# Down projections of the experts: from full-precision products to three fp32r products of split operands, in a one-core decoder layer

## The reference

```python
scores = softmax(x @ gate_w)                       # 8 experts, the best 2 kept and renormalised
for e in range(8):                                 # D = 256, H = 128
    hid = silu(x @ w_gate[e]) * (x @ w_up[e])      # [512, 256]
    y = y + w_per_expert[:, e:e+1] * (hid @ w_down[e])
shared = silu(x @ ws_gate) * (x @ ws_up) @ ws_down
out = x_residual + y + shared
```

## Time and profile before

| | us |
|---|---|
| Median of 3 runs | 206.36 |
| Range of the 3 runs | 206.1 to 208.32 |
| The profiled execution's own time | 206.29 |
| Its span, first to last instruction | 204.4 |
| TensorE busy in the span | 192.2 (94%) |
| VectorE busy | 157.7 (77%) |
| ScalarE busy | 137.1 (67%) |
| GpSimd busy | 97.4 (48%) |

### The profile page before, as it was taken

How to read it: one execution, slowest core, us unless ns; L and a number is a source line. 1 busy time by engine, 2 the same in 40 slices (tenths; PEclk the granted TensorE clock), 3 DMA queues, 4 the chain that set the end, 5 groups by cost and what they waited for, 6 DMA issues and landing times.

```text
span 204.4 us, 4606 instructions
## 1 busy us (share of the span) xinstructions
PE 192.2 (94%) x1626; PEld 150.7 (74%) x1626; DVE 157.7 (77%) x417; ACT 137.1 (67%) x316; POOL 97.4 (48%) x145
## 2 busy tenths in 40 slices
PE   7999996999999799996999999999989999999995
PEld 7688775678767567863666757576658799999994
DVE  2579989687669787579999999999983866458844
ACT  2499857797679749279998898987985332462220
POOL 7599207747673887905769991003400017500330
DMA  5980406801555104679514100000000000000001
GB/s 177 384 198 3 154 2 201 267 0 31 65 63 59 21 7 119 87 105 143 143 34 120 25 2 0 3 2 3 0 0 3 5 0 0 3 0 13 3 0 39
DMA packets 13286, 12.69 MB, mean 62 GB/s; under 512 B 1057, under 2 KB 11297, under 8 KB 13265
## 3 DMA queue, kind: packets, MB, share of 16 engines
q1 hardware_dynamic: 12160, 11.15, 24.2%
q10 hardware_dynamic: 1008, 1.06, 1.6%
q0 software_dynamic: 96, 0.20, 0.7%
HBM read 10.96 MB, written 1.44 MB: 61 GB/s over the span
## 4 chain that ended last, share of the span: by engine, by line
PE 63%; DVE 13%; ACT 10%; issue 6%; POOL 3%; DMA 3%; SPq 1%; DVEq 0%; POOLq 0%; ACTq 0%
PE ps L958 13%; PE ps L919 8%; PE ps L982 8%; PE ps L845 7%; PE ps L861 6%; PE ps L896 5%; PE ps L817 4%; PE ps L878 4%; DVE qk_low L1098 4%; ACT q_t L646 3%; PE ps L742 3%; DMA wk<-in_L_xattn_Wk 3%; DVE q_t L1186 2%; PE ps L936 2%; ACT place_k L646 2%
## 5 line engine op out<-in xcount | busy, mean ns | idle before, releaser
L1186 DVE CUSTOM_DVE_ANT_0 q_t<-ps,mask_add 128x512 f32<-128x512 f32 x64 | 41.4, 684 | 3.4 <-PE ps L878 2.2
L496 POOL TENSOR_TENSOR prob<-prob,rec 128x512 f32<-128x512 f32 x32 | 32.5, 1038 | 22.8 <-DVE rec L1245 22.8
L610 ACT ACTIVATE prob<-ps,low 128x256 f32<-128x256 f32 x64 | 29.8, 491 | 10.3 <-DVE low L1176 10.3
L646 ACT ACTIVATE q_t<-q_t,low 128x512 f32<-128x512 f32 x44 | 29.3, 717 | 4.2 <-DVE low L1186 4.1
L1176 DVE TENSOR_REDUCE low<-ps 128x2 f32<-128x512 f32 x32 | 20.4, 683 | 7.4 <-PE ps L817 7.3
L919 PEld LDWEIGHTS ps<-ident,q_t 128*128 128x128 f32 x176 | 19.6, 141 | 8.7 <-ACT q_t L646 2.9
L532 POOL TENSOR_TENSOR place_k<-place_k 128x256 f32<-128x256 f32 x10 | 7.3, 732 | 38.7 <-DVE place_k L1211 38.7
L919 PE MATMUL ps<-ident,q_t 128*128 128x128 f32 x176 | 23.7, 276 | 2.1 <-ACT place_k L682 0.8
L632 ACT ACTIVATE q_t<-ps 128x512 f32<-128x512 f32 x18 | 10.6, 599 | 21.1 <-PE ps L958 21.1
L1232 DVE TENSOR_TENSOR q_t<-q_t,ps 128x512 f32<-128x512 f32 x18 | 12.2, 685 | 11.4 <-PE ps L958 8.2
L861 PE MATMUL ps<-ident,prob 128*128 128x128 f32 x128 | 18.6, 279 | 2.2 <-POOL prob L496 0.9
(11 more groups left out here) (179 smaller groups left out, 471.7 us busy)
## 6 DMA issues: line engine op xcount, KB each, us to landing
k_stack<-k_dram SPq DMA_DIRECT2D x18, 128.0 KB
wg<-in_L_ffn_w_gate SPq DMA_DIRECT2D x1, 1024.0 KB, 5.5
wu<-in_L_ffn_w_up SPq DMA_DIRECT2D x1, 1024.0 KB, 8.0
q_stack<-q_dram SPq DMA_DIRECT2D x6, 144.0 KB
k_dram<-prob SPq DMA_DIRECT2D x1, 768.0 KB, 3.6
w_in<-in_L_attn_Wq ACTq DMA_DIRECT2D x2, 256.0 KB, 5.5
context<-in_ctx SPq DMA_DIRECT2D x1, 512.0 KB, 5.8
w_in<-in_L_attn_Wv SPq DMA_DIRECT2D x1, 512.0 KB, 7.5
```

What stands on the lines that cost most here:

```text
L496: nc.gpsimd.tensor_tensor(pr, pr, rec1[:, s % 2, r, :].unsqueeze(2).to_broadcast([P, C, S]), ALU.mult).then_inc(s_norm1, 1)
L610: e = nc.scalar.activation(prob1[:, s % 3, r, c * S:(c + 1) * S], ps[:, 2 * (s % 2) + r, c * S:(c + 1) * S], ACT.Exp, bias=low1[:, s % 2, ...
L646: nc.scalar.activation(prob2[n % 3][:, c, :], score2[n % 2][:, c, :], ACT.Exp, bias=low2[:, n % 2, c:c + 1], scale=-1.0).then_inc(s_exp2, 1)
L1186: nc.vector.tensor_tensor_reduce(out=score2[n % 2][:, c, :], in0=ps[:, 2 * (n % 2) + c, :], in1=mask_add[:, c, :], scale=1.0, scalar=3e38, ...
```

## The change

The down projection is done in the way the gate and up projections already are. VectorE now writes the product of Silu and the up projection back into the up bank of PSUM (signal `s_prod`); ScalarE copies it to SBUF, rounded to fp32r, as the high part (`s_hidhi`); VectorE subtracts the high part from the bank and gets the low part (`s_hid`), after it has done `outputs` of step `i - 2`. GpSimd splits the nine down weights in `split_down`: eight of them from `n = 23` to 30, in the place where the keys of the first sequence lay, and the ninth (expert 7) at `i = 2` of the experts' stage. TensorE runs 2 chunks x 2 halves x 3 products = 12 fp32r matmuls of 128x128 by 128 columns instead of 4 float32 ones. The storage of the hidden parts is where the keys of the second sequence lay.

```diff
--- before.py
+++ after.py
@@ -240,10 +240,12 @@
         q2_rest = sb("q2_rest", [P, S])
         q2_parts = sb("q2_parts", [P, PARTS, S], BF16)
         qk1_low = retired("qk1_low", [P, B, 2, NP, S], F32R)
+        after_keys = retired("after_keys", [P, B, NE * 2 * FF], F32R)
         k2_stack = sb("k2_stack", [KSTACK, B, H2, SK], BF16)
         qk_parts = retired("qk_parts", [P, 2, 2, H1 * HD1], F32R)
         q2_stack = sb("q2_stack", [KSTACK, H2, T], BF16)
 
+        last_down = retired("last_down", [P, 2, FC, D], F32R)
         v2 = sb("v2", [P, B * KC, H2, CW])
         low2 = sb("low2", [P, 2, C])
         o_raw = sb("o_raw", [P, S])
@@ -266,7 +268,10 @@
 
         gate_w = sb("gate_w", [P, NE])
         silu = [q1_t[:, i, :] for i in (0, 1)]
-        hid = [q1_t[:, i, :].rearrange("p (f t) -> p f t", f=FC) for i in (2, 3, 4)]
+        wd_parts = [after_keys[:, 0, k * 2 * FF:(k + 1) * 2 * FF].rearrange("p (i f n) -> p i f n", i=2, f=FC)
+                    for k in range(NE)] + [last_down]
+        hid = [after_keys[:, 1, i * 2 * FC * S:(i + 1) * 2 * FC * S].rearrange("p (i f t) -> p i f t", i=2, f=FC)
+               for i in range(3)]
         y_part = [place_k1[:, 2 + i, 0:C * D].rearrange("p (c n) -> p c n", c=C) for i in (0, 1)]
         acc = place_k1[:, 0, :].rearrange("p (c n) -> p c n", c=NC_)
         y_out = place_k1[:, 1, :].rearrange("p (c n) -> p c n", c=NC_)
@@ -324,6 +329,7 @@
         s_g, s_u, s_silu, s_hid, s_y, s_ypart, s_acc = map(sem, (
             "s_g", "s_u", "s_silu", "s_hid", "s_y", "s_ypart", "s_acc"))
         s_ysum = sem("s_ysum")
+        s_prod, s_hidhi, s_wdparts = map(sem, ("s_prod", "s_hidhi", "s_wdparts"))
 
         def chunks(ap):
             return ap.rearrange("b (c p) d -> p (b c) d", p=P)
@@ -465,6 +471,16 @@
                     pool.wait_ge(s_wo, B)
                 split((wg, wu)[which][:, e, :], [t[:, :] for t in w_parts[which][e]]).then_inc(s_wparts, 1)
 
+
+            def split_down(k):
+
+                if k == 0:
+                    pool.wait_ge(d_wd, 32)
+                    pool.wait_ge(s_score2, C * H2)
+                elif k == NE:
+                    pool.wait_ge(s_pv2, B * NG)
+                split(wd[:, (k - 1) % (NE + 1), :, :], [wd_parts[k][:, i, :, :] for i in range(2)]
+                      ).then_inc(s_wdparts, 1)
 
             def add_bv2(first, count):
                 pool.wait_ge(s_ev["act"], evacuated(index_of("vx", 1))[1])
@@ -518,8 +534,12 @@
                         split_queries2()
                 if 0 <= n - SPLIT_N < 2 * (NE + 1):
                     split_weights(n - SPLIT_N)
+                elif 0 <= n - SPLIT_N - 2 * (NE + 1) < NE:
+                    split_down(n - SPLIT_N - 2 * (NE + 1))
             for i in range(N_FFN):
                 b, k = divmod(i, NE + 1)
+                if i == 2:
+                    split_down(NE)
                 for kind, row, _ in FFN_BETWEEN.get(i + LAG_D, ()):
                     if kind == "turned2":
                         split_tokens(row)
@@ -628,8 +648,13 @@
             def silu_step(i):
                 act.wait_ge(s_g, i + 1)
                 if i >= 2:
-                    act.wait_ge(s_hid, i - 1)
+                    act.wait_ge(s_prod, i - 1)
                 nc.scalar.activation(silu[i % 2], ps[:, i % 2, :], ACT.Silu).then_inc(s_silu, 1)
+                act.wait_ge(s_prod, i + 1)
+                if i >= 3:
+                    act.wait_ge(s_y, C * (i - 2))
+                nc.scalar.copy(hid[i % 3][:, 0, :, :], ps[:, 2 + i % 2, :].rearrange("p (f t) -> p f t", f=FC)
+                               ).then_inc(s_hidhi, 1)
                 for what in FFN_BETWEEN.get(i, ()):
                     between(what)
 
@@ -966,11 +991,12 @@
                     up(2 + i % 2, 1).then_inc(s_u, 1)
                 if i >= LAG_D:
                     j = i - LAG_D
-                    e = (j % (NE + 1) - 1) % (NE + 1)
+                    e = j % (NE + 1)
                     if j == 0:
                         pe.wait_ge(s_pt2a, N_CROSS)
                         pe.wait_ge(s_pt2b, N_CROSS)
-                        pe.wait_ge(d_wd, 32)
+                    if j <= NE:
+                        pe.wait_ge(s_wdparts, j + 1)
                     pe.wait_ge(s_hid, j + 1)
                     if j >= 2:
                         b, k = divmod(j - 2, NE + 1)
@@ -979,9 +1005,10 @@
                             pe.wait_ge(s_ysum, C * (b * (NE - BY_POOL) + max(k - BY_POOL, 0)))
                     for c in range(C):
                         for f in range(FC):
-                            last = mm(ps[:, y_bank(j, c), c * P:(c + 1) * P],
-                                      hid[j % 3][:, f, c * P:(c + 1) * P], wd[:, e, f, :],
-                                      start=f == 0, stop=f == FC - 1)
+                            for part, (hi, wi) in enumerate(BIG_PARTS):
+                                last = mm(ps[:, y_bank(j, c), c * P:(c + 1) * P],
+                                          hid[j % 3][:, hi, f, c * P:(c + 1) * P], wd_parts[e][:, wi, f, :],
+                                          start=f == 0 and part == 0, stop=f == FC - 1 and part == len(BIG_PARTS) - 1)
                         last.then_inc(s_y, 1)
                 for what in FFN_BETWEEN.get(i, ()):
                     between(what)
@@ -1227,13 +1254,14 @@
                 if i < N_FFN:
                     dve.wait_ge(s_silu, i + 1)
                     dve.wait_ge(s_u, i + 1)
-                    if i >= 3:
-                        dve.wait_ge(s_y, C * (i - 2))
-                    v.tensor_tensor(hid[i % 3], silu[i % 2].rearrange("p (f t) -> p f t", f=FC),
-                                    ps[:, 2 + i % 2, :].rearrange("p (f t) -> p f t", f=FC), ALU.mult
-                                    ).then_inc(s_hid, 1)
+                    v.tensor_tensor(ps[:, 2 + i % 2, :], silu[i % 2], ps[:, 2 + i % 2, :], ALU.mult
+                                    ).then_inc(s_prod, 1)
                 if i >= LAG_D:
                     outputs(i - LAG_D)
+                if i < N_FFN:
+                    dve.wait_ge(s_hidhi, i + 1)
+                    v.tensor_tensor(hid[i % 3][:, 1, :, :], ps[:, 2 + i % 2, :].rearrange("p (f t) -> p f t", f=FC),
+                                    hid[i % 3][:, 0, :, :].bitcast(F32), ALU.subtract).then_inc(s_hid, 1)
                 for what in FFN_BETWEEN.get(i, ()):
                     between(what)
```

## The result

| | before | after |
|---|---|---|
| Median, us | 206.23 | 218.97 |
| Runs, us | 205.86 to 208.32 (4) | 218.29 to 220.54 (4) |
| Profiled execution, us | 206.29 | 219.17 |
| Its span, us | 204.4 | 216.7 |
| TensorE / VectorE / ScalarE / GpSimd busy, us | 192.2 / 157.7 / 137.1 / 97.4 | 201.8 / 169.4 / 146.8 / 106.9 |

The ratio is 1.0617 with a 95% interval of 1.0572 to 1.0663, so 11.8 to 13.7 us more. Forecast were 220.0 us and a range of 213.5 to 224.

A forecast was written before the change was run, and what follows sets the result against it. The experts' stage was taken as bound by TensorE, its matmuls priced by weight loads. 206.29 us + 8.8 (TensorE) + 4.8 (stalls at gate_weights) + 0 (GpSimd) gave 219.9, so 220.0 us; range 213.5 to 224.

The forecast's parts named there:

- The bound: Experts' stage: TensorE has no idle time from 162 to 202 us, its weight loads busy 39.60 of 40.00 us.
- TensorE's part: Down projection: 12 fp32r matmuls at a load's pitch of 115 ns, 1.38 us instead of 0.89; +8.8 us over 18 steps.
- the forecast's sign of 1.33 to 1.42: Chain in the changed profile: 12 down-projection records take 1.33 to 1.42 us; 0.7 would mean A, 2.7 B.
- The hidden state's part: Product, rounding copy and subtraction: covered in steady state, but TensorE stalls behind VectorE's gate_weights; +4.8 us.
- the two blocks: gate_weights in the experts' stage: holds VectorE 4.1 us, twice; product, copy and subtraction wait behind it.
- hand count: Experts' stage: three engines' lists carried forward with assumed durations; stalls of 5.0 us, 0.2 of them there before.
- GpSimd's part: Nine splits of down weights, about 2.1 us each, 19 us in all, lie in GpSimd's idle time; cost 0.
- The sum: Whole kernel: 206.29 + 8.8 + 4.8 = 219.9 us by the profiled execution, so 220.0 by the median.
- What was to show it wrong: A step is wrong if the span up to 156 us changes over 0.5 us or TensorE never waits after 162.
- A: Down projection: cheaper load, pitch 59 ns, but VectorE does not catch up after its blocks; 216.3 us, chance 0.13.
- B: Down projection: narrow fp32r matmul at the float32 price, 222 ns, VectorE's stalls covered; 238 us, chance 0.16.
- C: Experts' stage: not slower, pitch 59 ns (under 74 needed) and the new hand-overs hidden; 203.1 us, chance 0.03.

The follow-up runs named there:

- experiments 7 and 8: Experiment 1 with 4 of the 12 matmuls of a step moving (7) or loading (8) 64 columns instead of 128; 216.05 and 211.12 us, one execution each.
- experiment 1: Changed kernel with the hidden state the old way, one product straight to SBUF, no copy or subtraction; 12 matmuls and splits stay; 215.25 us, ratio 1.041.
- experiment 3: Changed kernel without the low-high product, so 8 of 12 fp32r matmuls a step; 217.66 us, ratio 1.051.
- experiment 6: Changed kernel with all parts of the down projection in bf16 instead of fp32r, still three products; 216.43 us, ratio 1.046.
- experiment 2: Kernel before, with only GpSimd's nine splits of the down weights added and read by nobody; 207.17 us, ratio 1.0042.
- experiments 4: Experiment 1 with the high-high product alone: 4 fp32r matmuls a step, hidden state the old way; 201.62 us, ratio 0.977.

## Why the prediction was right

By its own steps:

- **The bound.** That the stage hangs on TensorE and there on the weight loads: shown by experiments 7 and 8, in the kernel of experiment 1.
- **TensorE's part.** Forecast +8.8 us, measured +7.7 (experiment 1). The mechanism was right and the pitch a little too high: 115 ns was taken, and 112 is what each further load costs, as at the router; the prediction's lower likely end, 111 ns, gave +8.0 us. The 1.29 us of a group of 12 in the chain, below the forecast's sign of 1.33 to 1.42, is too short by the edge of 0.05 us that the next group has (experiment 1). Of the 0.3 us that are left, most is in the tail, whose last three down projections grew from 2.90 to 3.98 us and not by three times 0.45.
- **The hidden state's part.** Forecast +4.8 us, measured +3.6, of it 3.2 with the two blocks as their condition, where the prediction put them. By place: at the turn of the last output it had 0.9 us and the profile 0.52, at step 4's up projection 1.15 and 0.73, at step 14's 2.0 and 1.43. The 0.6 us at the second layernorm's turn and the 0.35 around step 9 and at the end did not come as waits of TensorE. The idle times add up to 2.7 us; part of the rest is the slow start behind a wait, 6 matmuls in 0.98 us where 12 take 1.43. All three durations were right to 10 ns. The prediction's hand count also gave the direction that experiments 3 and 6 show: the cheaper TensorE's work, the more of the loss is VectorE's.
- **GpSimd's part.** The cost, 0, was right as far as the stage shows (experiment 2); the work was mis-sized. A split was counted as 128x512, while a down weight tile of one expert is 2 x 128 = 256 columns; a pair takes 1.13 us, not 2.1:

```profile
145.01 0.39 POOL L441 CAST after_keys<-wd 128x256 fp32r<-128x256 f32 x1
145.49 0.74 POOL L442 TENSOR_TENSOR after_keys<-wd,after_keys 128x256 fp32r<-128x256 f32 x1
```

- **The sum.** 7.7 + 3.6 = 11.3 us of stage against 13.6 forecast. The median's 12.7 is nearer to the forecast than its terms are, through the start (1.0 us in this execution) and what lies outside the span (2.5 us in the profiled execution of after, 1.9 in that of before), neither of which the prediction had. So the closeness of 220.0 to 219.0 is in part luck: both terms were too high, by 1.1 and 1.2 us, and 1.6 us from outside the stage made up for most of it. The cause of what lies outside the span is not settled.
- **What was to show it wrong.** "If the span up to 156 us changes by more than 0.5 us": it did, by 1.0, and it arises in the warm-up of this execution, not in a step of the change.
- **Rivals.** A's time, 216.3, was met by experiment 6 with 216.4, though by another reason (the type), and in part by the clock's fall, which the hand count did not have; B, at 238 us, is out, as the narrow fp32r matmul has one record and a load's pitch. C fails on both its conditions: the fp32r pitch is 112 ns, not under 74, and with a pitch of 57.5 ns (bf16) the kernel is still 10 us slower.

## What to carry to other kernels

Count weight loads, not passes over the moving columns, when a float32 matmul is to be replaced by several cheaper ones on 128 columns or fewer: here 4 matmuls had 8 loads, and three products had 12. Before an engine's work is cut, ask what the other engines would do if it were free: with TensorE's work equal to before (experiment 3) the stage was 10 us longer, some 3 of them by the clock that fell behind the waits, and the chain of waits ran through two short blocks of tiny chained operations on VectorE, which had come to stand before a path grown by one copy and one subtraction. What made the kernel faster was to take neither: one product, and the hidden state rounded by the operation that wrote it anyway, 201.6 us where a single fp32r product is exact enough.

## What was not expected of the hardware

- A wait can cost more than its length. After 2.8 us of idle TensorE the granted clock fell to 0.50 for about 3.4 us in experiment 3, 1.6 us on top of the wait, and in experiment 6 it fell during the wait of 3.2 us and stayed there for some 7 us. The profiled execution of after shows no such fall before 214 us (clock 0.998 over the span); another of its executions, with a mean clock of 0.980, had a span of 218.5 us where the others had 216.3 to 216.7.
- The same 34 warm-up records took 5.43 to 7.01 us from execution to execution.
- The gate and up projections, 12 matmuls on 256 columns, show 1.47 us behind 4, 8 or 12 narrow fp32r matmuls alike (experiments 4, 3 and 1) and 1.42 behind 8 float32 records. As the loads keep their pitch, a group's time in the chain divided by its count is not the pitch: 12 in 1.29 us looks like 107.5 ns, and the loads are 112 ns apart.
- An fp32r load of 128 columns costs 112 ns like a float32 one, one of 64 columns about 53 ns less, and a bf16 load and matmul of 128 columns 57.5 ns together.
